# Expert blocks in first-need order, last combination and stores inside the second expert stage, block tables by matrix products

## Chip, cores and metric

The kernel runs on one core of one Trainium2 chip. The metric is device time in microseconds (us), median of three runs. A second number for the same kernel is the span of one profiled execution, from its first to its last instruction; the rows below come from that execution.

## What is computed

A layer of 8192 tokens (32 sequences of 256) with 128 features: a routed feed-forward, a linear attention, and the same feed-forward again.

```python
x = x + 0.5 * ffn(layernorm(x))      # 8 experts, top 2 of them per token, and a shared expert
x = x + attn(layernorm(x))           # linear attention over the 32 sequences, 16 heads of 8
x = x + 0.5 * ffn(layernorm(x))

def ffn(x):
    top_v, top_i = top_k(x @ gate_w, 2)
    top_p = softmax(top_v)
    d_e = (silu(x @ Wg[e]) * (x @ Wu[e])) @ Wd[e]            # 128 -> 352 -> 128
    return sum over the two chosen e of top_p * d_e  +  (silu(x @ Sg) * (x @ Su)) @ Sd
```

## The kernel before

Tokens go in 16 groups of 512 (GT), four tiles of 128 each; group g holds its x in X3(g), a slice of the resident tensor X. Every multiplication is made in a high and a low f16 part. The program has five stages, and all engines meet at the end of each (phase_end, L253).

1. Routing of the first feed-forward (first_ffn on each engine): logits, the two best experts, and a place for each of the 2 x 8192 token rows. DVE's place (L1215) adds running counts per expert (base) to positions that TensorE sums; the row of a token goes to its expert's region of the DRAM tensor routed_rows by an indirect DMA that POOL issues (scatter, L479, L485: eight per group). After the last group, ends and tables (L1244, L1249) make from the eight counts the tables of the expert stage: which row of routed_rows block b starts at (row_i) and which expert it belongs to (exp_i, eb).
2. Expert stage (experts on each engine): 72 places for blocks of 256 rows (NBLK), of which 71 are worked; the 16384 rows fill 64 blocks and each expert's last one is partly filled. Blocks are in the order of the experts: all of expert 0, then all of expert 1. For block n: SP loads it into one of four buffers (load_block, L372, L386), once block n-4 is transposed; TensorE transposes it (L983), makes gate and up products (18 matmuls of 256 columns, block_gate_up) and the down product of block n-2 (18 of 128, block_down); ACT takes silu (L683), makes the high part (L688) and copies the result of block n-2 out (L696, L697); DVE copies the transposed block (block_in, L1297), works out where its rows go (L1299), makes the low part of block n-1 (block_low, L1142) and the product of block n (block_mult, L1292); POOL writes a dummy (carrier, L494) and issues two indirect DMAs (L496) that scatter the 256 result rows of 512 bytes into the DRAM tensor expert_results, in the order of the tokens. ACT reuses a result buffer when the scatter of two blocks before has landed (s_results).
3. Streams: for each group, the two result rows per token are loaded and added, weighted with PR, then attention, then the routing of the second feed-forward. ends and tables again.
4. Expert stage, as 2, with n from 72 on.
5. Last combination: when every scatter has landed, SP loads group after group of result rows (load_last, 512 KB) into four buffers YL, ACT weighs the second choice (weigh_last, L665), DVE adds both (combine_last, L1345) and SP stores the group (store, L420, 256 KB). SP's order is: four loads, then store g, load g+4.

The order of the work on an engine is the order in which its program is written. DVE's step in the expert stage, which the change touches, is:

```python
def step(n, v, ahead=True):
    if ahead:
        block_in(n + 1, (v + 1) % XE, n + 1 - n0)
    block_low(n - 1, 1 - u)
    block_mult(n, u)
```

TensorE's step n is: transposes of block n+1 (which wait until DVE has copied block n out of the same PSUM bank, L979), gate and up of n, down of n-2.

## Time and profile before

| | |
|---|---|
| device time, median of three runs | 1241.1 us (1237.2, 1241.1, 1242.37) |
| the profiled execution, span | 1240.9 us |
| TensorE, busy | 989.7 us (80%), 8996 matmuls |
| VectorE (DVE), busy | 896.8 us (72%) |
| ScalarE (ACT), busy | 669.6 us (54%) |
| GpSimd (POOL), busy | 843.8 us (68%) |
| granted TensorE clock, mean | 0.930 |
| DMA | 86.62 MB, mean 70 GB/s |

How to read it: the profiled execution lies within 0.2 us of the median, so the sum can be made against its span. A busy share is an average over five stages with different limits; the table by stage is in the first group of rows below. Matmuls overlap in the record (their ends are modelled), so a step of TensorE is best read from the starts of its instructions. "issue" as a releaser means that the profile shows nothing that the engine waited for. A row of the engine "POOLq" or "DVEq" is the sequencer of that engine: register work, drains, waits.

### The profile page before, as it was taken

To read this page: it belongs to the slowest core of one execution; us is meant where nothing else is said; L and a number is where in the kernel's file an instruction comes from. 1 tells how busy PE (TensorE), PEld (TensorE's weight loads), DVE (VectorE), ACT (ScalarE), POOL (GpSimd) and SP (SyncE) were. 2 spreads that over 40 slices of the span, in tenths; PEclk is the share of its full clock that TensorE was granted. 3 is DMA by queue.
4 is the path that set the end of the run, shared out by engine and by line. 5 is a ranking of instruction groups with operands and counts; after the bars stand their busy time and mean duration, and the time that the engine had idled before them with its cause. 6 is when DMAs were issued, how large, how long until landed. Compare 5 with 4: busy or idle time off the path is not lost. (4 is left out here: it accounts for less than half of the span.)

```text
span 1240.9 us, 31979 instructions
## 1 busy us (share of the span) xinstructions
PE 989.7 (80%) x8996; PEld 742.7 (60%) x8997; DVE 896.8 (72%) x2369; ACT 669.6 (54%) x1466; POOL 843.8 (68%) x872
## 2 busy tenths in 40 slices
PE   2657665999999927788888888888864999999940
PEld 1434344899989924455555555555543888899930
DVE  6778784676676745788888888888854666666748
ACT  4556642555555523466665656666331555555545
POOL 4677773777777845467787787778642677777750
PEclk9898996999999968999999999999966999999985
DMA  9411122222222221001111111100003222222229
GB/s 279 108 51 47 52 76 66 78 79 76 78 77 78 68 59 33 17 33 37 34 34 51 34 38 41 41 17 18 23 27 87 74 74 77 78 75 78 73 95 332
DMA packets 68607, 86.62 MB, mean 70 GB/s; under 512 B 13004, under 2 KB 56209, under 8 KB 68558
## 3 DMA queue, kind: packets, MB, share of 16 engines
q1 hardware_dynamic: 51278, 52.15, 14.5%
q0 software_dynamic: 17280, 33.87, 8.3%
q8 instruction: 25, 0.41, 0.1%
q14 instruction: 24, 0.20, 0.1%
HBM read 44.74 MB, written 43.04 MB: 71 GB/s over the span
## 5 line engine op out<-in xcount | busy, mean ns | idle before, releaser
L496 POOL DMA_INDIRECT expert_results<-ey,eidx x284 | 293.3, 1033 | 70.9 <-issue 69.6
L485 POOL DMA_INDIRECT routed_rows<-row,idx x256 | 255.2, 997 | 73.6 <-issue 70.2
L1142 DVE SCALAR_TENSOR_TENSOR ehT<-eh,ehT 128x768 f16<-128x768 f32 x142 | 136.1, 958 | 150.1 <-ACT ehT L688 150.1
L683 ACT ACTIVATE esil<-PSUM 128x768 f32<-128x768 f32 x142 | 115.1, 810 | 230.2 <-PE PSUM L826 224.6
L824 PE MATMUL PSUM<-eT,WGU 128*128 128x256 f16 x852 | 234.3, 275 | 1.4
L825 PE MATMUL PSUM<-eT,WGU 128*128 128x256 f16 x852 | 233.9, 275 | 0.0
L826 PE MATMUL PSUM<-eT,WGU 128*128 128x256 f16 x852 | 233.8, 274 | 0.0
L510 POOL TENSOR_TENSOR space<-qk,val 128x1152 f32<-128x1152 f32 x64 | 138.2, 2171 | 69.5 <-DVE shift L1192 48.7
L824 PE MATMUL PSUM<-WD,ehT 128*128 x852 | 161.0, 220 | 8.3 <-DVE ehT L1142 5.0
L825 PE MATMUL PSUM<-WD,ehT 128*128 x852 | 159.3, 220 | 0.0
L826 PE MATMUL PSUM<-WD,ehT 128*128 x852 | 158.8, 219 | 0.0
L945 PE MATMUL PSUM<-space,upto 128*128 128x320 f32 (+1 forms) x384 | 148.4, 496 | 9.6 <-DVE prod L1366 6.8
L1292 DVE SCALAR_TENSOR_TENSOR eh<-PSUM,esil 128x768 f32<-128x768 f32 x142 | 134.9, 950 | 8.1 <-ACT esil L683 8.1
L494 POOL TENSOR_TENSOR carrier<-ones 128x1 f32<-128x1 f32 x142 | 73.0, 514 | 72.6 <-ACT ey L697 72.6
L688 ACT ACTIVATE ehT<-eh 128x768 f16<-128x768 f32 x142 | 118.6, 835 | 2.5 <-DVE eh L1292 2.5
L945 PEld LDWEIGHTS PSUM<-space,upto 128*128 128x128 f32 x384 | 71.8, 193 | 59.7 <-issue 42.0
L1366 DVE TENSOR_TENSOR prod<-PSUM,qk 128x1152 f32<-128x1152 f32 x64 | 86.3, 1348 | 13.9 <-PE PSUM L947 9.3
L824 PEld LDWEIGHTS PSUM<-eT,WGU 128*128 x852 | 83.7, 98 | 18.8 <-issue 6.8
L824 PEld LDWEIGHTS PSUM<-WD,ehT 128*128 128x128 f16 x852 | 82.9, 97 | 14.3 <-issue 9.7
L1369 DVE TENSOR_REDUCE space<-prod 128x144 f32<-128x1152 f32 x64 | 86.6, 1353 | 5.8
L826 PEld LDWEIGHTS PSUM<-eT,WGU 128*128 x852 | 84.0, 99 | 10.4
L825 PEld LDWEIGHTS PSUM<-eT,WGU 128*128 x852 | 84.1, 99 | 7.3
(197 smaller groups left out, 2300.0 us busy)
## 6 DMA issues: line engine op xcount, KB each, us to landing
xe<-routed_rows SPq DMA_DIRECT2D x142, 130.0 KB, 2.1
space<-expert_results SPq DMA_DIRECT2D x32, 512.0 KB, 3.9
expert_results<-ey,eidx POOLq DMA_INDIRECT x284
X<-in_L_attn_x_dram SPq DMA_DIRECT2D x16, 256.0 KB, 4.6
routed_rows<-row,idx POOLq DMA_INDIRECT x256, 2.3
out_dram<-X SPq DMA_DIRECT2D x16, 256.0 KB, 4.3
routed_rows<-pad_rows SPq DMA_DIRECT2D x24, 130.0 KB
space<-in_L_ffn_Wg_dram SPq DMA_DIRECT2D x1, 1408.0 KB, 9.1
```

What stands on the lines that cost most here:

```text
L485: pool.indirect_dma_start(routed, bass.IndirectOffsetOnAxis(ap=idx[u][:, k, j:j + 1], axis=0), row[u][:, j, :], None).then_inc(s_scattered ...
L496: pool.indirect_dma_start(result, bass.IndirectOffsetOnAxis(ap=eidx[u][:, h:h + 1], axis=0), ey[u][:, h, :], None, bounds_check=K * T - 1, ...
L510: pool.tensor_tensor(kv[:, q, a, :].rearrange("p (h j i) -> p h j i", h=HEADS, j=VD), k4, v4, ALU.mult).then_inc(s_outer, 1)
L683: act.activation(esil[u][:, :], PSUM[:, 1536 * u:1536 * u + 768], ACT.Silu, scale=2.0 ** -(SX + SWT)).then_inc(s_block_silu, 1)
L688: act.activation(ehT[u][:, 0, :, :], eh32[u][:, :].rearrange("p (c t) -> p c t", c=NC), ACT.Copy).then_inc(s_block_high, 1)
L824: pe.matmul(dst, a[0], b[0], start=start, stop=False)
L825: pe.matmul(dst, a[0], b[1], start=False, stop=False)
L826: return pe.matmul(dst, a[1], b[0], start=False, stop=stop)
L945: mm = pe.matmul(PKV[:, lo:hi], upto[:, :], kv[:, q, a, lo:hi], start=True, stop=(a == 0))
L1142: return dve.scalar_tensor_tensor(out=dst, in0=src, scalar=float(2 ** scale), in1=high, op0=ALU.mult, op1=ALU.subtract)
L1292: dve.scalar_tensor_tensor(out=eh32[u][:, :], in0=PSUM[:, at:at + NC * BLK], scalar=2.0 ** (SH - SX - SWT), in1=esil[u][:, :], op0=ALU.mul ...
L1369: dve.tensor_reduce(num[:, j, :, :], prod[:, a, :].rearrange("p (h j i) -> p h j i", h=HEADS, j=VD), AX.X, ALU.add)
```

## The change

**Tables.** The running counts are kept for every group (counts, 17 sets of 8, instead of base). For each pair of a group and an expert, the blocks that this group is the first to need are counted (fresh), pairs are ordered by group, then by expert, and two products on TensorE turn that into the starting row and the expert of each block. DVE's serial sum over eight experts and its four operations on 72 x 8 elements are gone; in their place stand three transposes and six products on TensorE, three round trips between the engines. TensorE does its part before down(14) in the first routing and before the last down in the second (tables(0), tables(1)).

**Last combination.** With blocks in this order, all result rows of group g are in DRAM when a first part of the blocks is through (COMPLETE + 1 + 4 g of them, in the code's terms). In the second expert stage SP loads and stores groups between block loads (merged), and DVE adds two pieces of a group per step: 128 x 128 of the first choice ahead of block_low, 128 x 128 of the second choice behind block_mult, after a drain. Four steps make a group; groups 0 to 12 are made in 52 steps, groups 13, 14 and 15 after the stage's end. ACT no longer weighs anything at the end.

```diff
+MERGED = 12
+COMPLETE = 10
...
+            def landed(g):
+
+                if not isinstance(g, int):
+                    sp.wait_ge(s_block_results, g * NJ + (NBLK + COMPLETE + 3))
+                    return
+                for u in range(2):
+                    sp.wait_ge(s_results[u], 16 * HALVES * (NBLK // 2 - u + COMPLETE // 2 + 1 - u + g * (NJ // 2)))
+
+            def merged(g, u, stored=True):
+                landed(g)
+                load_last(g, u)
+                if stored:
+                    store(g - 2)
...
-            for u in range(LAST):
-                load_last(u, u)
-            with sp.Fori(0, NG // LAST - 1) as i:
...
+            with sp.Fori(0, MERGED // LAST - 1) as i:
                 for u in range(LAST):
-                    store(i * LAST + u)
-                    load_last(i * LAST + (LAST + u), u)
-            for u in range(LAST):
-                store(NG - LAST + u)
+                    for v in range(XE):
+                        block_of(i * (LAST * XE) + (NBLK + 2 * LAST * XE + u * XE + v), v)
+                        if v == 2:
+                            merged(i * LAST + (LAST + u), u)
...
+            sp.drain().then_inc(s_phase, 1)
+            for g in range(MERGED + 2, NG):
+                merged(g, g % LAST)
+            for g in range(NG - 2, NG):
+                store(g)
             sp.wait_ge(s_stored, 16 * NG)
...
+            def tables(f):
+
+                pe.wait_ge(s_fresh, f + 1)
+                pe.transpose(PT[:, 0:P], fresh[:, :], ident[:, :])
+                pe.transpose(PT[:, P:2 * P], expert_step[:, :], ident[:, :]).then_inc(s_fresh_turned, 1)
+                pe.wait_ge(s_fresh_T, f + 1)
+                pe.matmul(SUM_BEFORE, turned[:, 0:P], before[:, :], start=True, stop=True)
...
+                pe.wait_ge(s_offsets_T, f + 1)
+                pe.matmul(SUM_OFFSET, offset_turned[:, :], past[:, :], start=True, stop=True).then_inc(s_block_sums, 1)
...
-                dve.tensor_tensor(base[:, :], base[:, :], pos[:, NJ, :], ALU.add)
+                dve.tensor_tensor(counts[:, cols(g, E, E)], old, pos[:, NJ, :], ALU.add)
...
-                def step(n, v, ahead=True):
+                def step(n, v, ahead=True, merge=None):
                     u = v % 2
                     if ahead:
                         block_in(n + 1, (v + 1) % XE, n + 1 - n0)
+                    if merge is not None:
+                        combine_last(*merge, 0)
                     block_low(n - 1, 1 - u)
                     block_mult(n, u)
+                    if merge is not None:
+                        dve.drain()
+                        combine_last(*merge, 1)
...
+                plain = LAST if f else (NBLK - 4) // XE
+                with dve.Fori(0, plain) as i:
                     for b in range(XE):
                         step(i * XE + (n0 + 2 + b), (2 + b) % XE)
+                if f:
+                    with dve.Fori(0, MERGED // LAST) as i:
+                        for g in range(LAST):
+                            for b in range(XE):
+                                step(i * (LAST * XE) + (n0 + LAST * XE + 2 + g * XE + b), (2 + b) % XE, merge=(i * LAST + g, g, b))
...
+            def combine_last(g, u, j, k):
+
+                if j == 0 and k == 0:
+                    dve.wait_ge(s_YL[u], (g - u) * (16 // LAST) + 16)
+                x1 = X3(g)[:, j, :]
+                last = dve.scalar_tensor_tensor(out=x1, in0=YL[u][:, j, k, :], scalar=PR[:, cols(g, NJ * K, j * K + k, 1)],
+                                                in1=x1, op0=ALU.mult, op1=ALU.add)
+                if j == NJ - 1 and k == K - 1:
+                    last.then_inc(s_combined, 1)
...
             phase_end(dve, 4)
-            with dve.Fori(0, NG // LAST) as i:
-                for u in range(LAST):
-                    combine_last(i * LAST + u, u)
+            for g in range(MERGED + 1, NG):
+                for k in range(K):
+                    for j in range(NJ):
+                        combine_last(g, g % LAST, j, k)
+                    dve.drain()
```

Two places show how the order moves. ISA and REGISTER_ALU rows are the sequencer's work on addresses and counters.

DVE, second expert stage, one step of the loop before (copy of the transposed block, its places, low part, product, and the copy of the next):

```order
L1297 COPY eT<-PSUM 128x512
L1299 ISA
L1299 SCALAR_TENSOR_TENSOR places<-xe,eb 128x2
L1142 SCALAR_TENSOR_TENSOR ehT<-eh,ehT 128x768
L1292 SCALAR_TENSOR_TENSOR eh<-PSUM,esil 128x768
L1296 REGISTER_ALU
L1297 COPY eT<-PSUM 128x512
```

DVE, the same step in the changed kernel's merging loop (X<-space,PR,X is a piece of the combination; space holds YL):

```order
L1350 COPY eT<-PSUM 128x512
L1352 ISA
L1352 SCALAR_TENSOR_TENSOR places<-xe,eb 128x2
L1416 ISA
L1416 SCALAR_TENSOR_TENSOR X<-space,PR,X 128x128
L1202 SCALAR_TENSOR_TENSOR ehT<-eh,ehT 128x768
L1345 SCALAR_TENSOR_TENSOR eh<-PSUM,esil 128x768
L1416 ISA
L1416 SCALAR_TENSOR_TENSOR X<-space,PR,X 128x128
L1349 REGISTER_ALU
L1350 COPY eT<-PSUM 128x512
```

One piece stands ahead of the low part, the other (with a drain that makes no row here) between the product and the copy of the next transposed block.

SP, second expert stage before: two block loads of the loop (xe), nothing between them:

```order
L251 REGISTER_ALU
L385 ISA
L385 TENSOR_LOAD row_i
L385 ISA x2
L386 ISA
L386 DMA xe<-routed_rows 128x260
```

SP in the changed kernel, between the third and the fourth block load of each four:

```order
L400 DMA xe<-routed_rows 128x260
L442 ISA
L413 ISA
L413 DMA space<-expert_results 128x1024
L435 REGISTER_ALU
L436 ISA
L436 DMA out_dram<-X 128x4x128
L265 REGISTER_ALU
L399 ISA
L399 TENSOR_LOAD row_i
L399 ISA x2
L400 ISA
```

A load of 512 KB and a store of 256 KB, each behind a wait, now stand in SP's queue ahead of every fourth block load.

## Rows read from the trace of the kernel before

**Rows 1.** Stages: from, to, length, busy us of each engine, PEclk, DMA share, GB/s.
```profile
197.90:450.90 253.00, 239.53 (x2840) 214.59 (x2840) 162.53 (x284) 137.28 (x284) 183.54 (x213) 0.97 0.25 71
...
947.40:1202.10 254.70, 240.33 (x2840) 213.97 (x2840) 162.93 (x285) 137.28 (x284) 182.66 (x213) 0.98 0.25 71
1202.10:1240.90 38.80, 0.00 (x0) 0.00 (x0) 28.76 (x80) 20.54 (x64) 0.00 (x0) 0.50 0.93 325
```

**Rows 2.** Timeline of DVE in the last stage (start, us, operation).
```profile
1209.74 1.13 DVE L1350 SCALAR_TENSOR_TENSOR X<-space,PR,X 128x128 f32 x4
1211.02 0.69 DVE L1354 TENSOR_TENSOR X<-X,space 128x512 f32 x1
...
1237.53 0.69 DVE L1354 TENSOR_TENSOR X<-X,space 128x512 f32 x1
```

**Rows 3.** Line 491, POOL's drain at a stage's last block: min/median/max ns, starts.
```profile
L491 POOLq DRAIN  x2: 4491/4779/5067, 448.5 to 1198.5; - x2
```

**Rows 4.** Timeline of DVE, start of stage 3: eight pieces of one group.
```profile
455.53 2.36 DVE L1339 SCALAR_TENSOR_TENSOR X<-space,PR,X 128x128 f32<-128x128 f32 x8 [1.93 <-DMA space<-expert_results]
```

**Rows 5.** Timeline of DVE, second expert stage, one step.
```profile
1062.82 0.41 DVE L1297 COPY eT<-PSUM 128x512 f16<-128x512 f16 x1
...
1064.31 0.96 DVE L1142 SCALAR_TENSOR_TENSOR ehT<-eh,ehT 128x768 f16<-128x768 f32 x1 [0.95 <-ACT ehT L688]
1065.19 0.95 DVE L1292 SCALAR_TENSOR_TENSOR eh<-PSUM,esil 128x768 f32<-128x768 f32 x1
1066.06 0.41 DVE L1297 COPY eT<-PSUM 128x512 f16<-128x512 f16 x1
```

**Rows 6.** Timeline of TensorE around the same step: its transposes.
```profile
1063.54 0.39 PE L983 MATMUL PSUM<-ident,xe 128*128 128x128 f16 x4
...
1066.97 0.39 PE L983 MATMUL PSUM<-ident,xe 128*128 128x128 f16 x4
```

**Rows 7.** Eight blocks of the second expert stage, columns as in rows 1.
```profile
1046.34:1073.07 26.73, 26.64 (x324) 23.84 (x321) 18.29 (x33) 15.34 (x33) 20.52 (x25) 1.00 0.27 77
```

**Rows 8.** POOL's timeline: a usual step, then steps behind a late one.
```profile
1064.73 0.59 POOL L494 TENSOR_TENSOR carrier<-ones 128x1 f32<-128x1 f32 x1 [0.21 <-ACT ey L697]
1065.47 1.00 POOL L496 DMA_INDIRECT expert_results<-ey,eidx  x1 [0.15 <-issue]
1066.78 0.98 POOL L496 DMA_INDIRECT expert_results<-ey,eidx  x1 [0.30 <-issue]
...
1155.60 0.98 POOL L496 DMA_INDIRECT expert_results<-ey,eidx  x1 [2.26 <-issue]
...
1161.37 1.50 POOL L496 DMA_INDIRECT expert_results<-ey,eidx  x1 [0.31 <-issue]
1162.86 0.24 POOL L494 TENSOR_TENSOR carrier<-ones 128x1 f32<-128x1 f32 x1
```

**Rows 9.** Waits of ACT, stages 2 to 4: us in total, times, longest.
```profile
ACT eidx L696 <- DMA expert_results<-ey,eidx: 4.7, 5, 2.0
```

**Rows 10.** Line 485, scatters of stages 1 and 3, issue to landing.
```profile
DMA to landing us min/median/max: 2.3/2.3/5.8
```

**Rows 11.** DMA issues of the last stage: count, KB each, median us to landing.
```profile
space<-expert_results SPq DMA_DIRECT2D x16, 512.0 KB, 5.0
```

**Rows 12.** Timeline of DVE, end of stage 3: first and last of the tables.
```profile
935.21 0.15 DVE L1251 TENSOR_TENSOR nb<-base,region 128x8 f32<-128x8 f32 x1
...
942.81 0.19 DVE L1285 CAST exp_i<-eb 128x72 int32<-128x72 f32 x1
```

**Rows 13.** The chain of waits from stage 3 into stage 4: start, us, what.
```profile
944.46 0.95 POOL routed_rows L485
...
946.95 3.34 POOLq L255
...
950.89 0.60 PE PSUM L983 x4
```

**Rows 14.** Line 1241: sequencer work on an address, min/median/max ns.
```profile
L1241 DVEq FUSED_REGOPS  x14: 57/57/76, 56.0 to 824.2; - x14
```

More of the change, by code:

```diff
@@ L125, in macaron @@
         block_no = sb("block_no", [P, NBLK])
-        base = sb("base", [P, E])
+        counts = sb("counts", [P, (NG + 1) * E])
         base_i = sb("base_i", [P, E], I32)
@@ L412, in _ @@
                     sp.wait_ge(s_scattered[v], scattered(f, v))
-                fours(sp, f * NBLK, (f + 1) * NBLK, load_block(f))
-                sp.drain().then_inc(s_phase, 1)
-                for u in range(2):
-                    sp.wait_ge(s_results[u], 16 * HALVES * (NBLK // 2 - u) * (f + 1))
                 if f == 0:
+                    fours(sp, 0, NBLK, load_block(0))
+                    sp.drain().then_inc(s_phase, 1)
+                    for u in range(2):
+                        sp.wait_ge(s_results[u], 16 * HALVES * (NBLK // 2 - u))
                     pairs(sp, 0, NG, load_results)
@@ L663, in weigh @@
                 last.then_inc(s_weighed, 1)
-            def weigh_last(g, u):
-                act.wait_ge(s_YL[u], (g - u) * (16 // LAST) + 16)
-                for j in range(NJ):
-                    last = act.activation(YL[u][:, j, 1, :], YL[u][:, j, 1, :], ACT.Copy,
-                                          scale=PR[:, cols(g, NJ * K, j * K + 1, 1)])
-                last.then_inc(s_weighed, 1)
             def residual(m):
@@ L1072, in first_ffn @@
                     pe.wait_ge(s_weights_low, 2)
+                if edge and n == NG - 1:
+                    tables(0)
                 if not edge or n > 0:
@@ L1105, in streams @@
                         qkv_products(m + 2, 1, a)
+                if isinstance(m, int) and m == NG:
+                    tables(1)
                 if settle:
@@ L1246, in ends, with tables @@
                 dve.drain()
-                dve.tensor_copy(base_i[:, :], base[:, :]).then_inc(s_row_ends, 1)
-            def tables():
-                dve.tensor_tensor(nb[:, :], base[:, :], region0[:, :], ALU.subtract)
-                dve.drain()
-                dve.tensor_scalar(nb[:, :], nb[:, :], float(BLK - 1), None, ALU.add)
+                dve.tensor_copy(base_i[:, :], counts[:, NG * E:(NG + 1) * E]).then_inc(s_row_ends, 1)
+            def tables(f):
+                dve.tensor_scalar(nb[:, :], counts[:, :], float(BLK - 1), None, ALU.add)
                 dve.drain()
@@ L1322, in experts @@
                 block_mult(n0 + 1, 1)
-                with dve.Fori(0, (NBLK - 4) // XE) as i:
+                plain = LAST if f else (NBLK - 4) // XE
+                with dve.Fori(0, plain) as i:
                     for b in range(XE):
                         step(i * XE + (n0 + 2 + b), (2 + b) % XE)
+                if f:
+                    with dve.Fori(0, MERGED // LAST) as i:
+                        for g in range(LAST):
+                            for b in range(XE):
+                                step(i * (LAST * XE) + (n0 + LAST * XE + 2 + g * XE + b), (2 + b) % XE, merge=(i * LAST + g, g, b))
+                    for b in range(XE):
+                        step(n0 + (LAST + MERGED) * XE + 2 + b, (2 + b) % XE, merge=(MERGED, 0, b))
                 step(n1 - 2, 2, ahead=False)
@@ L1425, in first_ffn @@
                     ends()
-                    tables()
+                    tables(0)
                 shared(n, 0)
@@ L1470, in _ @@
             dve.wait_ge(s_constants, 1)
-            dve.tensor_copy(base[:, :], region0[:, :])
+            dve.tensor_copy(counts[:, 0:E], region0[:, :])
             dve.wait_ge(s_second_tokens, 32)
@@ L1506, in streams @@
                         ends()
-                        tables()
+                        tables(1)
                     shared_low(n - 1)
```

100 lines of the change are left out of this document (61 added, 39 removed).

## The prediction

> **What bounds the kernel now.** I read the table by stage first. The last stage, in which TensorE and POOL do nothing, takes 38.8 us with the DMA engines 0.93 busy, and the two expert stages 253.0 and 254.7 us [rows 1] with DMA at 0.25: work of a loaded resource stands alone where the stages beside it leave it idle. Within an expert stage I then read eight blocks as one window: 26.73 us, so 3.34 per block, of which TensorE is busy 26.64, DVE 18.29, ACT 15.34 and POOL 20.52 [rows 7]. TensorE looks like the bound, but its matmul records overlap, so I checked by single steps how much later the others could be. DVE's timeline shows 0.95 us of idleness ahead of the low part, and none from the low part over the product to the copy of the next transposed block, which starts at 1066.06 and ends at 1066.47 [rows 5]. TensorE's next transposes wait for that copy and start at 1066.97; one step earlier the copy ended at 1063.23 and the transposes started at 1063.54 [rows 5, 6]. The slack is 0.3 to 0.5 us: a stage bound by TensorE, with DVE's chain right behind. The third view is POOL's timeline: it waited 0.21 us for ACT ahead of its dummy in a usual step, and after one issue that came 2.26 us late it no longer waits at all [rows 8]. So POOL is close behind too.
>
> **The last stage.** Removed are the 16 groups of loads, additions and stores, 38.8 us from the landing of the last scatter to the end [rows 1]. Put back are groups 13 to 15. DVE may not start them before all engines have met, and POOL comes last there: its drain begins at 1198.5 and takes 5.07 us [rows 3], to 1203.6; I take DVE's start as 1203.9. One group is eight pieces in 2.36 us [rows 4] and about 0.15 for the last drain (four pieces of 1.13 from 1209.74, the next operation at 1211.02: 0.15 behind them [rows 2]), 2.5 in all. Three make 7.5, to 1211.4. The load of group 15 starts when the last scatter has landed, at 1202.1, and with even 5.0 us [rows 11] is there by 1207.1, before DVE reaches it at 1208.9. From DVE's last operation to the end it was 2.7 us (1238.22 [rows 2] to 1240.9) and stays so. The end is then 1214.1: a gain of 26.8 us. The 13 other groups' loads and stores lie beside the expert stage.
>
> **What the merged steps cost.** In 52 of the 71 steps DVE makes two pieces more. The first stands in the 0.95 us of idleness [rows 5]; a piece takes 0.28 (1.13 / 4 [rows 2]), some 0.35 with its tail, and is covered, though with the copy coming later (below) only some 0.1 us of the cover is left. The second piece is on the chain: the product's start to the copy's start was 0.87 (1065.19 to 1066.06 [rows 5]); now it is 0.95 for the product to end, 0.15 of drain gap and 0.28, so 1.38, or 0.5 later. The slack was 0.3 to 0.5 less some 0.13 that a release takes (my estimate from the 0.1 to 0.15 between operations that follow each other), so 0.17 to 0.37. What is over, 0.13 to 0.33 us, delays the transposes of the block after next, so it is spread over two steps: 0.07 to 0.17 per block, 3.6 to 8.6 us over 52 steps. TensorE's clean step is shorter than the mean one of 3.34, and its own pauses take up some of it; I take 5.0, with 0 and 8.6 as the ends.
>
> **POOL and the scatters.** The dummy took 0.59 us with DVE's low part running beside it and 0.24 without, a scatter 1.50 against 0.98, and each time the longer one ends behind the end of the low part (1065.27; in the late steps likewise) [rows 5, 8]. So POOL is held up while DVE runs an operation on two SBUF inputs, and the new pieces are of that kind. This is the rule in the Trainium skill, SBUF — State Buffer, Who interferes with whom: a DVE instruction with two SBUF inputs and a GpSimd instruction that reads SBUF shut each other out for their whole length. The row agrees with the rule, and the rule speaks against the change. By itself it would have POOL lose both pieces in every step, which is the third case below; what the row adds is that a step loses only what meets a start. POOL's step is 0.24 + 0.15 + 1.00 + 0.30 + 0.98 without any of it, 2.7 us, and 3.0 with one hold-up, against 3.34; one more of 0.3 fits. I take 1 us for this, between 0 and 14.
>
> Beside that, the load of 512 KB and the store of 256 KB per group now share the DMA engines with the scatters. ACT waits for a scatter two blocks later; it did so 5 times for 4.7 us in all [rows 9]. Scatters landed in 2.3 us as a median and 5.8 at most [rows 10]; the second one of a block is issued at 1066.78 [rows 8], so it lands at 1069.1, and ACT, whose copy-out ended just ahead of the dummy at 1064.73, needs the buffer for the copy-out two steps or 6.7 us later, at about 1071: some 1.8 us are spare. I take 1 us, between 0 and 10. SP's queue: the fourth block load of each four stands behind a wait for a result, a load and a store. The wait is for the result of a block six places ahead of the last one loaded; that load itself was allowed when the block four places ahead was transposed, and its result comes two steps behind its transposes. So the fourth load comes about one step later than before; with four buffers it had three steps in hand, and the 0.77 MB in front of it take some 5 us of the rest. Nothing.
>
> **Tables and counts.** DVE's tables took 7.8 us (935.21 to 943.00 [rows 12]). The new ones have about 14 small operations at 0.25 us from start to start and three round trips over TensorE; I take 5.5 to 6 us. Neither is on the path: the stage ends with POOL's last scatter, at 945.41, its landing and POOL's drain of 3.34, while TensorE starts the next stage at 950.89 [rows 13]. The cover is POOL's eight scatters; without it the gain would be 2 us at either end of a routing. The pads and TensorE's down product, which stand behind the tables, come no later. So 0, for both. The running count now needs an address in each loop: 0.06 us [rows 14], once per group in 24 of 32 groups, 1.4 at most, 0.5 taken. POOL's two memsets and one iota more at the start are 0.7 us by the dummy's 0.24 [rows 8]; DVE and ACT normalize the first group meanwhile, so 0. The order of the blocks itself changes no duration: every block reads its expert by a register, before as after.
>
> **Sum.** 1240.9 - 26.8 + 5.0 + 1 + 1 + 0.5 = 1221.6 us. The executed profile stands 0.2 us under the median, which I leave out: 1221.5.
>
> **Rivals.** (a) The pieces are nearly free: TensorE's own pauses hide the 0.13 to 0.33 us, since DVE has 8 us of idleness in each eight blocks [rows 7]. Against it stands that this idleness lies in one place. Costs of 0 to 3: 1214 to 1217, say 1216. (b) POOL becomes the bound of the merged steps: with 3.3 us as in the late steps and one hold-up of 0.28 more, 3.6 per block, 0.26 x 52 = 14 us, with the address work 1229. For it: the late steps of 1155 and after, where POOL has no slack. (c) The pieces hold POOL up twice in every step, the low part does too, and the scatters land late behind the 768 KB: POOL needs 2.7 + 0.5 + 2 x 0.35 = 3.9 us per block, 0.56 x 52 = 29 us more than now. 1214.1 + 29 + 4 of landing = 1247, slower than before. It decides from 3.34 + 26.8 / 52 = 3.86 us per merged step. Against it: POOL's three reads and DVE's three long operations would all have to meet, in steps of one length. (d) The change does not do what it says: SP comes to its loads too late, DVE waits for YL in the middle of its loop, and the groups cost in the stage what they cost behind it. The load is issued some three steps ahead of its use and takes 5 us [rows 11] of 10, so it should not. It would bring half the gain back: 1235.
>
> **Chances and range.** My forecast (costs of 4 to 11 us, 1218 to 1225) 0.48; (a) 0.22; (b) 0.21; (c) 0.04; (d) 0.05. A measurement of this kernel tells 0.5% or 6.2 us from no change: faster is below 1234.9. That is the forecast, (a) and (b) whole, and a little of (d): 0.93; same 0.04, slower 0.03. The range takes in (a) and (b), down to all costs nought and up to POOL's case with 4 us of late scatters; since the three runs before lay up to 4 us under their median, it begins 2 us lower: 1212 to 1233.
>
> **What would show it.** In the changed profile: the last stage from the last scatter's landing to the end near 12 us, with three groups of eight pieces; DVE's piece behind the product 0.28 us and the copy starting 1.3 to 1.4 us behind the product's start; eight merged blocks as a window in 27.2 to 28.2 us; the 16 unmerged first ones as before; ACT's waits for scatters under 1 us per group. Wrong would be shown by waits of DVE for the loads of YL, by POOL without any wait for ACT in all merged steps at over 3.5 us, by TensorE waiting for the copy by over 0.3 us per step, and by the expert stage starting later behind the tables.

## The result, and the profile after

The changed kernel takes 1230.7 us as the median of four runs (1228.3 to 1232.5), the kernel before 1241.7 beside it: a ratio of 0.9926, 95% interval 0.9906 to 0.9945. The forecast of 1221.5 had the sign right and promised a gain of 19.6 us, where 11.0 came. The executed profile of the changed kernel is its quickest run, 1228.3 us with a span of 1226.5; as in every run here the time is some 1.8 us over the span. So the span before, 1240.9, stands for a time of 1242.7, 1 us over the median and not within 0.2 of it as was said there; the forecast gain isn't touched by this, but the two profiles lie 14.4 us apart where the medians lie 11.0. Where single runs took over 1.5% longer at a lower granted clock, as one of e4's six (1268.1 us), the ratios leave them out.

The windows by stage of the changed kernel, columns as in [rows 1]:

```profile
197.40:452.70 255.30, 240.49 (x2840) 214.99 (x2840) 162.55 (x284) 137.46 (x284) 183.23 (x213) 0.96 0.24 70
...
948.30:1214.95 266.65, 249.86 (x2840) 212.60 (x2840) 194.89 (x388) 136.92 (x284) 180.72 (x213) 0.97 0.36 110
1214.95:1226.50 11.55, 0.00 (x0) 0.00 (x0) 6.83 (x24) 0.00 (x0) 0.00 (x0) 0.50 0.36 114
```

Against [rows 1] the last stage fell from 38.8 to 11.55 us, and the second expert stage grew from 254.7 to 266.65, with DVE's busy time up by 32 us (104 pieces). All that lies outside these two stages is 0.9 us longer in this profile. The same 2840 matmuls of TensorE are busy 249.86 us in place of 240.33, so its idleness grew by only 2.4 us (16.8 against 14.4): where the ends of matmuls are modelled, a busy share doesn't show where 12 us are lost.

The timeline of DVE in two merged steps does (start, us, operation, in brackets the idle time before it and its releaser), beside [rows 5]:

```profile
1111.00 0.96 DVE L1202 SCALAR_TENSOR_TENSOR ehT<-eh,ehT 128x768 f16<-128x768 f32 x1 [0.36 <-ACT ehT L731]
1111.88 0.95 DVE L1345 SCALAR_TENSOR_TENSOR eh<-PSUM,esil 128x768 f32<-128x768 f32 x1
1113.03 0.35 DVE L1416 SCALAR_TENSOR_TENSOR X<-space,PR,X 128x128 f32 x1 [0.20 <-issue]
1113.29 0.42 DVE L1350 COPY eT<-PSUM 128x512 f16<-128x512 f16 x1
1113.63 0.21 DVE L1352 SCALAR_TENSOR_TENSOR places<-xe,eb 128x2 f32 x1
1113.76 0.34 DVE L1416 SCALAR_TENSOR_TENSOR X<-space,PR,X 128x128 f32 x1
1114.55 0.96 DVE L1202 SCALAR_TENSOR_TENSOR ehT<-eh,ehT 128x768 f16<-128x768 f32 x1 [0.45 <-ACT ehT L731]
```

The first piece (1113.76) is covered; DVE still waits 0.45 us for ACT behind it. The second (1113.03) is on the chain: the copy starts 1.41 us behind the product's start (1111.88), where it was 0.87. From ACT's silu of step 18 to that of step 66 of the second expert stage, counted from 0, the changed kernel takes 170.1 us, 3.545 a block, the kernel before 159.6, 3.325; these rows are the two ends of it:

```profile
1017.28 0.81 ACT L726 ACTIVATE esil<-PSUM 128x768 f32<-128x768 f32 x1 [1.78 <-PE PSUM L866]
...
1187.42 0.81 ACT L726 ACTIVATE esil<-PSUM 128x768 f32<-128x768 f32 x1 [1.41 <-PE PSUM L866]
```

0.22 us a block in 52 steps is 11.4 us. The waits of the changed kernel in that window (us in total, times, longest):

```profile
ACT esil L726 <- PE PSUM L866: 78.1, 48, 1.9
POOL carrier L545 <- ACT ey L740: 23.5, 44, 0.9
...
DVE ehT L1202 <- ACT ehT L731: 21.6, 48, 1.1
PEld PSUM L864 <- issue: 11.6, 37, 0.5
```

and of the kernel before in the same 48 steps:

```profile
POOL carrier L494 <- ACT ey L697: 13.0, 41, 0.7
...
PEld PSUM L824 <- issue: 1.8, 5, 0.4
```

POOL waits for ACT more than before, 23.5 against 13.0 us, so it sets no pace. No wait of DVE for YL appears, and none of ACT for a scatter. TensorE's pauses without a releaser were 5 and are 37, and all of them stand ahead of the tenth of the 18 weight loads of gate and up, where its queue loads the number of the next expert from memory (line 1047, between the gate and the up products):

```profile
1118.95 0.10 PEld L864 LDWEIGHTS PSUM<-eT,WGU 128*128 x1 [0.45 <-issue]
```

```profile
L1047 PEldq TENSOR_LOAD <-exp_i x142: 295/303/802, 200.0 to 1196.9; - x142
```

The load's 0.30 us was there before too. The reading is that the queue then had it behind it before the array needed the next product, and released later has not; e10 below tests it.

The end is what was forecast: the last load at 1214.95, POOL's drain, three groups of eight pieces, their stores.

```profile
1214.95 0.33 SPq L413 DMA_DIRECT2D space<-expert_results  x1
1216.54 7.25 DVE L1416 SCALAR_TENSOR_TENSOR X<-space,PR,X 128x128 f32<-128x128 f32 x24 [9.52 <-POOLq L269]
1218.93 5.27 SPq L436 DMA_DIRECT2D out_dram<-X  x3
```

### The profile page after: what moved, and what is told of

Its sections match the earlier page's. It is cut to its first block and busy times, and to the rows that moved or that the text cites. A ratio compares the mean times of both kernels' runs of the same rounds, so it can differ in the third digit from the quotient of the medians.

```text
span 1226.5 us, 31850 instructions
## 1 busy us (share of the span) xinstructions
PE 1002.4 (82%) x9014; PEld 744.1 (61%) x9015; DVE 901.5 (73%) x2403; ACT 649.2 (53%) x1402; POOL 839.6 (68%) x875
## 5 line engine op out<-in xcount | busy, mean ns | idle before, releaser
L547 POOL DMA_INDIRECT expert_results<-ey,eidx x284 | 288.6, 1016 | 71.2 <-issue 65.5
L536 POOL DMA_INDIRECT routed_rows<-row,idx x256 | 252.5, 986 | 73.5 <-issue 69.4
L864 PE MATMUL PSUM<-WD,ehT 128*128 x852 | 164.5, 220 | 9.5 <-ACT ey L740 5.5
L865 PE MATMUL PSUM<-WD,ehT 128*128 x852 | 161.8, 221 | 0.0
L866 PE MATMUL PSUM<-WD,ehT 128*128 x852 | 161.3, 220 | 0.0
```

The lines of the kernel that those rows point to most:

```text
L536: pool.indirect_dma_start(routed, bass.IndirectOffsetOnAxis(ap=idx[u][:, k, j:j + 1], axis=0), row[u][:, j, :], None).then_inc(s_scattered ...
L547: pool.indirect_dma_start(result, bass.IndirectOffsetOnAxis(ap=eidx[u][:, h:h + 1], axis=0), ey[u][:, h, :], None, bounds_check=K * T - 1, ...
L864: pe.matmul(dst, a[0], b[0], start=start, stop=False)
L865: pe.matmul(dst, a[0], b[1], start=False, stop=False)
L866: return pe.matmul(dst, a[1], b[0], start=False, stop=stop)
```

## The experiments

Ratios are to the kernel before on the same chip, with 95% intervals. "Step" is the time per block from the silu of step 18 to that of 66, as above. Three of the five sets (e5 to e8, e13 to e16, e17 and e18) ran on chips on which every kernel, the one before too, took some 11 to 12% longer; these have a part of their own.

**e1: both pieces ahead of the low part.**

```diff
 combine_last(*merge, 0)
+dve.drain()
+combine_last(*merge, 1)
 block_low(n - 1, 1 - u)
 block_mult(n, u)
-if merge is not None:
-    dve.drain()
-    combine_last(*merge, 1)
```

> The changed kernel with both pieces of the last combination ahead of VectorE's low part, in the time in which it waits for ScalarE anyway (0.45 us there in the changed kernel with one piece in it), so that nothing stands between the product and the next copy. Same number of pieces, same transfers, same tables. Theory 1 (the second piece makes the copy 0.54 us later, and TensorE's sequencer, not its array, runs out of lead): the copy starts 0.9 us behind the product's start again as before the change, the merged steps go back from 3.545 to 3.33 to 3.38 us a block, and the time falls from 1230.7 to 1220 to 1224 us. Rival (the pieces' transfers, the lock between VectorE and GpSimd, or VectorE's total of work slow the steps, wherever the pieces stand): the pace stays at 3.5, 1229 to 1232 us.

Measured: 1221.5 us, 0.9837 (0.9814 to 0.9861), step 3.368. Its DVE, one step:

```profile
1111.27 0.95 DVE L1345 SCALAR_TENSOR_TENSOR eh<-PSUM,esil 128x768 f32<-128x768 f32 x1
1112.13 0.41 DVE L1350 COPY eT<-PSUM 128x512 f16<-128x512 f16 x1
1112.46 0.21 DVE L1352 SCALAR_TENSOR_TENSOR places<-xe,eb 128x2 f32 x1
1112.60 0.34 DVE L1415 SCALAR_TENSOR_TENSOR X<-space,PR,X 128x128 f32 x1
1113.12 0.35 DVE L1415 SCALAR_TENSOR_TENSOR X<-space,PR,X 128x128 f32 x1 [0.17 <-issue]
1113.58 0.96 DVE L1202 SCALAR_TENSOR_TENSOR ehT<-eh,ehT 128x768 f16<-128x768 f32 x1
```

The copy is back at 0.86 behind the product. The same pieces and transfers at another place cost 0.04 us a block in place of 0.22, as theory 1 expected. DVE's wait for ACT is just used up by the two in this step. This kernel beats both kernels of the study, and has the lowest ratio of all that ran on chips like the first (e9's interval overlaps with its own).

**e2: the transfers without the pieces.** Seven of eight pieces of 13 groups are left out, so the combination is incomplete.

```diff
-    combine_last(*merge, 0)
...
-if merge is not None:
+if merge is not None and merge[2] == NJ - 1:
     dve.drain()
     combine_last(*merge, 1)
...
```

The piece that is left also makes DVE's wait for the load of the group.

> The changed kernel in which seven of eight pieces of each merged group are left out (the combination of 13 groups is incomplete); the last piece of each group stays as the signal for the store, so all loads and stores go on inside the expert stage as in the changed kernel. Theory 1: with a late copy in one step of four, 3.33 to 3.42 us a block, 1219 to 1223 us. Rival (the transfers of the merged groups slow the steps by contention): 3.5 us a block, 1229 to 1231 us.

Measured: 1227.7 us, 0.989 (0.9872 to 0.9908), step 3.480. Read by its time alone this would speak for the rival: it lies over theory 1's 1219 to 1223 us and just under the rival's 1229 to 1231, the step between both. The timeline says otherwise: the one piece left comes later than it did among eight, with 0.43 us of idleness for no releaser ahead of it (0.20 in the changed kernel), and the copy starts 1.64 us behind the product:

```profile
1092.39 0.95 DVE L1345 SCALAR_TENSOR_TENSOR eh<-PSUM,esil 128x768 f32<-128x768 f32 x1
1093.77 0.35 DVE L1414 SCALAR_TENSOR_TENSOR X<-space,PR,X 128x128 f32 x1 [0.43 <-issue]
1094.03 0.42 DVE L1350 COPY eT<-PSUM 128x512 f16<-128x512 f16 x1
```

From silu to silu, as means over the 48 steps by their place among four, beginning with the one in which the late copy lies:

```
us                   late copy     next    third   fourth    sum
before                   3.373    3.300    3.205    3.423  13.30
e2                       3.959    3.361    3.221    3.381  13.92
```

The loss of 0.62 us in four steps follows the one late copy (0.59, and 0.06 in the step behind it), and the other two run as before with all transfers going on. So the transfers are cleared, but by the timeline and e1, not by this time.

**e3: the kernel before with one piece on scratch memory**, in 52 steps of the second expert stage. No transfers, order and tables of before.

```diff
 block_mult(n, u)
+if piece:
+    dve.drain()
+    dve.scalar_tensor_tensor(out=prod[:, 0, 0:D], in0=prod[:, 0, 0:D],
+                             scalar=PR[:, 0:1], in1=prod[:, 0, D:2 * D],
+                             op0=ALU.mult, op1=ALU.add)
```

> The kernel before with one thing added: in 52 steps of the second expert stage VectorE makes a drain and one scalar_tensor_tensor of 128x128 on scratch memory behind the product, where the changed kernel has its second piece; no transfer, no new order, no new tables. Theory 1: the whole loss comes from this place alone, 0.18 to 0.24 us a step, 1241 + 9 to 12 = 1250 to 1253 us. Rival (transfers, order or tables): the added 0.45 us goes into the slack that the trace shows at TensorE, 1241 to 1243 us.

Measured: 1251.1 us, 1.0079 (1.006 to 1.0097), step 3.511, the copy 1.32 to 1.46 behind the product, and 34 pauses of TensorE ahead of the same tenth weight load. So a piece at this place, with no transfer and no new order or table, brings 0.19 of the 0.22 us; the rest is about what e1 still loses.

**e4: tables and order alone.** The changed kernel with the last stage of before (stores, combination and ACT's weighing behind the expert stage).

> The changed kernel's tables and order of the blocks, with the last combination and the stores behind the second expert stage as before. Theory 1: the order costs nothing in the steps, 3.32 to 3.34 us a block in both expert stages, and the tables nothing that is seen behind GpSimd's scatters: 1239 to 1242 us, as before the change. Rival (the new order, with its steps of expert number from block to block, makes the expert steps slower): 0.2 us more a block in the second stage, 1249 us or more.

Measured: 1245.9 us, 1.0041 (1.0025 to 1.0058), step 3.323. The order costs nothing in the steps, as expected; but the kernel is 3 to 7 us slower, which theory 1 had excluded, and not at the place that the rival named. From the last silu of the first expert stage to the first of the second it is 522.0 us against 518.7. In that middle stage the running count now stands at an address that depends on the group. The first three operations of place, in the kernel before:

```profile
757.50 0.19 DVE L1219 TENSOR_TENSOR posb<-PSUM,base 128x32 f32<-128x32 f32 x1 [1.26 <-PE PSUM L945]
757.76 0.16 DVE L1221 TENSOR_TENSOR base<-base,PSUM 128x8 f32<-128x8 f32 x1
757.84 1.12 DVE L1223 TENSOR_TENSOR pk<-pick,posb 128x64 f32<-128x64 f32 x1
```

and in e4:

```profile
758.14 0.19 DVE L1258 TENSOR_TENSOR posb<-PSUM,counts 128x32 f32<-128x32 f32 x1 [1.36 <-PE PSUM L979]
758.50 0.16 DVE L1260 TENSOR_TENSOR counts<-counts,PSUM 128x8 f32 x1 [0.17 <-issue]
758.58 1.08 DVE L1262 TENSOR_TENSOR pk<-pick,posb 128x64 f32<-128x64 f32 x1
```

```profile
775.00:776.00 1.00, 0.67 (x8) 0.49 (x9) 0.91 (x2) 0.85 (x5) 0.69 (x2) 1.00 0.01 4
776.00:777.00 1.00, 1.00 (x4) 0.51 (x3) 1.00 (x4) 1.00 (x6) 0.69 (x2) 0.57 0.19 62
777.00:778.00 1.00, 1.00 (x3) 0.67 (x2) 0.85 (x8) 1.00 (x5) 0.94 (x1) 0.50 0.20 67
778.00:779.00 1.00, 1.00 (x3) 0.67 (x2) 0.70 (x5) 0.98 (x3) 0.75 (x1) 0.50 0.19 67
779.00:780.00 1.00, 1.00 (x3) 0.53 (x2) 0.69 (x5) 0.99 (x2) 0.22 (x1) 0.72 0.19 67
```

Such a group, with a mean granted clock of 0.94, is in the profiles of the changed kernel, of e1, e9 and e10 (once each) and of e2 (twice), and not in those of the kernel before and e3, where it is 1.00. So it goes with the tables and counts; what makes the clock fall there is not shown.

A later group of the stage, in which the clock falls in the kernel before too, goes the other way. It has the same 88 matmuls in each kernel, before and changed (columns as in [rows 1]):

```profile
893.41:919.67 26.26, 17.47 (x88) 9.68 (x88) 16.63 (x51) 7.41 (x17) 9.05 (x10) 0.74 0.06 21
897.46:921.66 24.20, 14.69 (x88) 8.63 (x88) 16.62 (x51) 7.40 (x17) 9.08 (x10) 0.84 0.07 23
```

In e10 it has a clock of 0.91 and takes 22.9 us, in e4 0.74 and 26.3. So kernels with the same tables differ by up to 8 us between the two silus: e10 516.3, e9 518.4, the changed kernel 519.2, e4 522.0, e1 522.5, e2 524.4. One profile each doesn't tell how much of this is chance.

**e9: copies one block further ahead.** VectorE copies block m + 2 in step m, in its idle time ahead of the low part; the pieces stay.

```diff
-block_in(n + 1, (v + 1) % XE, n + 1 - n0)
+block_in(n + 2, (v + 2) % XE, n + 2 - n0)
```

(with the first and last steps of the loops shifted by one). 

> The changed kernel with VectorE's copies one block further ahead, once more, since the first time all kernels, the one before too, took 12% longer on that chip. In terms of the kernel before on the same chip: theory 1 (the chain of one step over the copy is cut) 0.982 to 0.985, the merged steps at 3.32 to 3.36 us where the kernel before has 3.33; the rival (the total of the pieces or the transfers) 0.990 to 0.994.

Measured: 1223.8 us, 0.9865 (0.9844 to 0.9886), between theory 1 and the rival. The steps without pieces became shorter than those of before (steps 18 to 66 of the first expert stage 3.290 against 3.313), the merged ones hardly, 3.537, where theory 1 expected 3.32 to 3.36. Its timeline shows a new chain:

```profile
1101.90 0.39 PE L1039 MATMUL PSUM<-ident,xe 128*128 128x128 f16 x4
1102.33 0.42 DVE L1350 COPY eT<-PSUM 128x512 f16<-128x512 f16 x1 [0.39 <-PE PSUM L1039]
...
1102.80 0.34 DVE L1415 SCALAR_TENSOR_TENSOR X<-space,PR,X 128x128 f32 x1
1103.06 0.95 DVE L1202 SCALAR_TENSOR_TENSOR ehT<-eh,ehT 128x768 f16<-128x768 f32 x1
...
1105.34 0.39 PE L1039 MATMUL PSUM<-ident,xe 128*128 128x128 f16 x4
```

Transposes, copy, places, first piece, low part, the down products that wait for it, next transposes: 3.44 us. By this reading the first piece is now on a chain. That is not shown: the kernels for it (e13, e17 below) ran on no chip like the first.

**e10: the expert's number loaded behind the up products.**

```diff
 for W, o in ((WG, 0), (WU, NC * BLK)):
-    if o and ahead is not None:
-        read_number(ahead, v)
...
 mm.then_inc(s_block_products, 1)
+if ahead is not None:
+    read_number(ahead, v)
```

> The changed kernel with the load of the next expert's number behind the up products, once more for the same reason. Theory 2 (the load sits in the chain of one step) 0.985 to 0.989 of the kernel before; if the late copy sets the pace wherever the load stands, 0.992 to 0.995. On the slower chip, whose queues show pauses everywhere, it had 0.967 where the changed kernel with another small edit had 0.987; that this is a gain of the slower chip alone would show here as 0.992.

Measured: 1226.8 us, 0.9883 (0.986 to 0.9905), step 3.500. A fifth of the loss of 0.22 comes back, 2.3 us in 52 steps of the 3.9 by which the medians differ. None of TensorE's pauses stands ahead of the tenth weight load of gate and up any more; 26 stand ahead of the down products. So the load is a part of the chain, the smaller one.

**e11 and e12: a fixed address for the counts, and all three edits.**

```diff
 def place(n, u, g):
+    dve.tensor_copy(counts[:, cols(g, E)], base[:, :])
     dve.wait_ge(s_positions, n + 1)
...
-    dve.tensor_tensor(counts[:, cols(g, E, E)], old, pos[:, NJ, :], ALU.add)
+    dve.tensor_tensor(base[:, :], base[:, :], pos[:, NJ, :], ALU.add)
```

> The changed kernel with both pieces ahead of the low part and, beside that, the running counts in a tile of fixed address, copied to the table in VectorE's idle time. The first alone had 0.984 of the kernel before. Theory 3 (the register work in the middle of place costs 2 to 4 us of the middle stage): 0.981 to 0.982 and no group of 29.2 us in the middle stage. Rival (it comes from elsewhere): 0.984.

> Both pieces ahead of the low part, counts in a tile of fixed address, and the load of the next expert's number behind the up products. If all three theories hold: 0.978 to 0.981 of the kernel before, below both kernels of this study; if the load only matters where the copy is late, it adds nothing to the other two, 0.981 to 0.983.

Measured: e11 1232.7 us, 0.9941 (0.9925 to 0.9957), step 3.367; e12 1228.1, 0.9907 (0.9888 to 0.9927), step 3.382. Both miss what was expected (0.981 to 0.984 and 0.978 to 0.983). Against e1 the fixed address made it worse. The middle groups take 27.8 us, with two and three of 29.1 to 29.5. The copy went to the wrong place: DVE's idle time is ahead of a wait for the running sums that stands before place, so the copy lies behind it.

```profile
627.28 0.55 DVE L1277 COPY counts<-base 128x8 f32 x1 [1.17 <-PE PSUM L1002]
627.75 0.18 DVE L1281 TENSOR_TENSOR posb<-PSUM,base 128x32 f32<-128x32 f32 x1
```

The copy and its address put 0.47 us between the release and the addition. It tells that DVE's chain bounds the middle stage and passes such a delay on, and nothing on theory 3. The load's place adds nothing once the copy is in time (3.382 against 3.367).

**On the slower chips.** There the kernel before took 1393 us (e5 to e8), 1374 (e13 to e16) and 1394 (e17, e18).

> The changed kernel with VectorE's copies one block further ahead in both expert stages: step m copies block m + 2 (not m + 1) before the low part of m - 1 and the product of m, so the copy that TensorE's next transposes wait for is done in VectorE's idle time and not behind the product and the second piece. Both pieces stay at their places. Theory 1 (a chain of one step: gate and up of m, silu, low part, product, second piece, copy of m + 1, transposes of m + 2, gate and up of m + 1; each step pays for the second piece anew): the chain is cut, 3.32 to 3.36 us a block in the merged steps, 1218 to 1223 us. Rival (not the copy but the total of the pieces or the transfers slow TensorE): 3.5 us a block, 1229 to 1232 us.

> The kernel before with the same change of VectorE's order in both expert stages and nothing else. TensorE was busy 159.1 of 159.6 us in 48 steps of the kernel before, so theory 1 expects nothing or the few tenths left there: 1238 to 1242 us. Rival (the copy already limits the steps of the kernel before, and the full array is only an effect of how ends are modelled): 0.1 us a block in 142 blocks, 1228 us or less.

> The changed kernel in which TensorE's queue loads the number of the next block's expert behind the up products and not between the gate and the up products; everything else as in the changed kernel. Theory 2 (the pauses of TensorE in the middle of gate and up, 0.24 us a step, are the register load that the queue no longer makes in time, and they are part of the chain of one step): without them 3.40 to 3.47 us a block, 1223 to 1227 us. Rival (the load only shows where the array runs dry, the late copy sets the pace wherever it stands): 3.5 us a block or more, 1229 to 1233 us.

> The changed kernel in which the running counts of place are kept in a tile of fixed address, as before the change, and are copied to the table of counts at an address by group in VectorE's idle time ahead of the wait for the positions. In the middle stage with the tables the groups took 27.5 us (27.4 before the change), and in each of four profiles one or two of them 29.2 with a drop of TensorE's clock in it; the kernel before and the one with a piece added to it show none. Theory 3 (the register work in the middle of place, 0.17 us of idleness there, is what puts 2 to 4 us on the middle stage): 1226.5 to 1229 us, no group of 29.2 us. Rival (the 4 us of the tables and the order come from elsewhere): 1230 to 1232 us.

Measured, as ratios: e5 (the edit of e9) 0.9893 (0.9848 to 0.9939), e6 (the same on the kernel before) 1.0025 (0.9992 to 1.0058), e7 (the edit of e10) 0.9674 (0.9622 to 0.9726), e8 (the fixed address alone) 0.9873 (0.9815 to 0.9932). The changed kernel did not run there, so e8 is the nearest to it.

> The changed kernel with VectorE's copies one block further ahead (as in the kernels copy_ahead) and both pieces behind the product, where VectorE now waits for the next transposes. With one piece ahead of the low part the merged steps had stayed at 3.54 us although the copy was off its old place, and the trace showed a new chain: transposes of m + 2, copy, places, first piece, low part, down products that wait for it, next transposes, 3.44 us. If that is the cause, taking the first piece out of it (0.26 us) lets TensorE's array set the pace: 3.29 to 3.33 us a block in merged and other steps, 0.977 to 0.981 of the kernel before, below both kernels. Rival (transfers or the total of VectorE's work keep the merged steps slow in this order): 3.45 to 3.54 us, 0.986.

> The changed kernel with both pieces ahead of the low part, and in place the update of the counts (with the register work for its address) behind the product of picks and positions and not ahead of it, so that GpSimd's index tile waits for the same number of operations but the address work lies beside one of them. Theory (the 0.09 us more from the positions' addition to that product is what makes the middle groups 27.5 and not 27.4 us): 27.4 us a group, 0.982 to 0.984 of the kernel before, against 0.984 for the one without this edit. Rival (the order does not matter, since the address work stands on VectorE's chain either way): no difference, 27.5 us a group.

> Both of the last two edits together: copies one block further ahead with both pieces behind the product, and the counts updated later in place. If both theories hold 0.975 to 0.980 of the kernel before; if only the first does, as that kernel alone.

> The kernel before with the piece on scratch memory behind the product doubled (drain and two scalar_tensor_tensor of 128x128 in 52 steps), so that the copy comes about 0.74 us later than before the change, after 0.46 with one piece (0.186 us a block lost) and 0.54 in the changed kernel (0.22 lost). A chain over two steps (copy of a block, its transposes' successor, gate and up, silu, low part, product, piece, copy of the block after next) with 0.1 us of slack loses half of what is over: (0.74 - 0.10) / 2 = 0.32 us a block, 1.013 to 1.014 of the kernel before. A chain over one step with 0.3 us of slack loses all of it: 0.44 us a block, 1.018 to 1.019.

> Copies one block further ahead and both pieces behind the product, once more, since the first time every kernel took some 11% longer on its chip and TensorE's queue paused in all of them. On a chip like the first: 3.29 to 3.33 us a block in merged and other steps, 0.977 to 0.981 of the kernel before. If the merged steps stay at 3.45 us or more, the chain over the first piece was not the cause, 0.986.

> The kernel before with two pieces on scratch memory behind the product in 52 steps, once more for the same reason. A chain over two steps with 0.1 us of slack: 0.32 us a block over the 3.33 of before in the merged steps, 1.013 to 1.014. A chain over one step with 0.3 us of slack: 0.44 us a block, 1.018 to 1.019.

Measured: e13 0.9857 (0.9815 to 0.99), e14 0.9719 (0.9669 to 0.9768), e15 0.9872 (0.9828 to 0.9915), e16 1.004 (1.0006 to 1.0073), e17 0.9837 (0.9804 to 0.9871), e18 1.0045 (1.001 to 1.008). The edits of the first two are

```diff
-combine_last(*merge, 0)
 block_low(n - 1, 1 - u)
 block_mult(n, u)
+combine_last(*merge, 0)
 dve.drain()
 combine_last(*merge, 1)
```

on top of e9, and on top of e1, in place,

```diff
-dve.tensor_tensor(counts[:, cols(g, E, E)], old, pos[:, NJ, :], ALU.add)
 dve.tensor_tensor(pk[:, :, :, :], pick[:, :, :, :], pb, ALU.mult)
 dve.drain()
...
+dve.tensor_tensor(counts[:, cols(g, E, E)], old, pos[:, NJ, :], ALU.add)
```

e15 has both, e17 is e13 again; e16 and e18 are e3 with a second piece behind the first. None of them decides what it was made for: steps take 2.5 to 7.0 us in one and the same loop (e18), and the means hide tenths. The two-piece kernel has 4.149 us a step in e18, and its 1.004 and 1.0045 miss both theories (1.013 to 1.014 and 1.018 to 1.019); why it loses less than e3 did on the first kind of chip is not shown. What these sets do show is in the last section.

## Why the prediction was wrong

**The last stage** was right: 11.55 us against "near 12", a gain of 27.2 against 26.8.

**The merged steps** are the step that failed: 5.0 us taken (0 to 8.6 as ends), 11.4 measured. Its parts can be read from the traces, as means over 44 to 46 of these steps, from the starts of the copy, the next transposes (T), the silu behind them, the product behind that, and the copy behind that:

```
us                  copy to T  T to silu  silu to product  product to copy    sum
before                  0.911      2.420            2.449            0.868  6.648
e1 (pieces ahead)       0.953      2.446            2.450            0.868  6.717
e3 (before + piece)     0.698      2.529            2.450            1.358  7.036
changed                 0.659      2.563            2.451            1.430  7.103
e10 (load later)        0.725      2.391            2.451            1.430  6.997
```

The sum is two steps in each kernel (before 2 x 3.325, changed 2 x 3.55): the chain returns to the copy after two steps. So "spread over two steps" was right, and the expectations of e5 and e9, which speak of a chain of one step, have this wrong; e16 and e18, made to settle it, weren't needed for it. "0.5 later" was right (0.56). The slack was 0.25 us in the gap between copy and transposes (0.911 to 0.659), inside the 0.17 to 0.37 that [rows 5, 6] had given. By these alone the loss is (0.56 - 0.25) / 2 x 52 = 8.1 us, near the upper end; the 5.0 came of letting "its own pauses take up some of it", for which no row stood, and that was the first fault. The second is a term that was put at nothing: the stretch from T to silu was taken as fixed and grew by 0.143 us, 3.7 us in 52 steps. That is the register load that the queue makes while the array waits: with the load moved, e10 has 2.391. Slack was read where the array starts; the queue in front of it had less. 8.1 + 3.7 is 11.8, beside 11.4 measured. The signs named for a wrong forecast did not tell it: DVE never waited for YL in these steps, POOL waited for ACT in 44 of 48, TensorE for a copy once, 0.2 us. Only the eight merged blocks, 28.4 us (8 x 3.545), lay just outside the 27.2 to 28.2.

e2 fits the same chain. Even and odd blocks are two chains side by side, so a piece in each step costs once per two steps (0.455), four steps 0.91. A single copy 0.77 us late in four steps costs 0.62, all but 0.15; that it does so on its own chain alone is argued, not shown.

**POOL and the scatters**, 1 + 1 us: nothing of it is seen. POOL's wait for ACT grew by 10.5 us, and in the whole second expert stage ACT waited once, 1.4 us, for a scatter. The mutual exclusion that the Trainium skill states (SBUF — State Buffer, Who interferes with whom) may still lengthen single operations. The dummy takes 0.56 us as a mean in that stage, in place of 0.53, a scatter 1.00 in place of 1.03, and nothing shows in their sum: POOL is busy 180.72 us in the second expert stage in place of 182.66 [rows 1], with 104 more operations of DVE beside it, and e1 has the same pieces at 0.04 us a step. POOL does not set the pace here, so this has no price.

**Tables and counts**, 0 + 0.5 us: 3 to 7 measured in e4, 0.5 in the changed kernel's own profile. The tables are in fact hidden. From the first to the last of them DVE takes 5.5 us, with POOL's scatters going on for over 4 us more and its drain behind (timeline of DVE, then the chain of waits):

```profile
936.68 0.22 DVE L1312 TENSOR_SCALAR nb<-counts 128x136 f32<-128x136 f32 x1
...
941.95 0.26 DVE L1338 CAST exp_i<-eb 128x72 int32<-128x72 f32 x1
```

```profile
945.77 0.96 POOL routed_rows L536
...
948.22 3.34 POOLq L269
```

What failed in e4 is the address of the counts: its 0.06 us [rows 14] was priced right, twice in place and at 0.10 together, at most 1.5 us in the stage, but not the clock drop of 1.8 us that goes with it, nor some 0.7 us more in one of the last groups (27.4 in place of 26.8). That is up to 4.0, where e4's profile is 3.3 longer there. The changed kernel has all of this too, but its late group got 2.1 us back at a clock of 0.84 in place of 0.74. So the middle stage of its profile is only 0.5 us longer (519.2 against 518.7), and whether its other runs paid as e4's did is not shown.

Together: in the two profiles -27.25 for the last stage, +11.95 for the second expert stage and +0.9 for the rest are the 14.4 us between the spans. By the medians, 1241.8 - 27.2 + 11.4 + 3.8 (e4's five runs other than that of 1268.1 us, against before) = 1229.8, beside 1230.7; that it comes so near is in part luck, since the 3.8 is e4's. Of the rivals, (a) is what e1 does, not this kernel; (b) and (c) fall with POOL's waits, (d) with the missing waits for YL. That (b) named nearly the right time, 1229, was an accident of its price.

Open stay: what makes the clock fall in the middle stage, and so what tables and counts cost from run to run; whether the first piece holds e9's merged steps; whether a later update of the counts helps.

## What to carry to other kernels

Slack read at an engine's array is not the slack of its queue: where the queue works out addresses or loads registers within the stretch, a later release lengthens the stretch itself, so add that work to the delay or test it with an operation on scratch memory (e3). Before a small piece is put into a loop, follow each chain of waits until it returns to itself and put the piece where its engine waits for something that is not on that chain: here 0.04 in place of 0.22 us a step, for two moved lines. When a kernel without the suspected work is still slow, look at where the remaining work went before believing it (e2).

## What the runs showed of the hardware

- The kernel before took 1241 to 1242 us on two chips and 1374 to 1394 on three others, with the same durations of single operations: a low part 0.95 to 0.96 us on either kind. The same edit ran on both kinds in e9 (1221.3 us in its profile) and e5 (1375.6). Of the 154 us between them 47 lie ahead of the first silu, 50 and 53 in the expert stages and 4 in the middle. What grew most are pauses ahead of TensorE's weight loads for which no releaser shows, those of line 864 in e9 and in e5:

```profile
PEld PSUM L864 <- issue: 28.4, 52, 3.6
```

```profile
PEld PSUM L864 <- issue: 148.5, 159, 6.0
```

  In e17 they come back at the same places of TensorE's loop of eight steps; these two are 33.9 us or eight steps apart:

```profile
1180.34 0.10 PEld L864 LDWEIGHTS PSUM<-WD,ehT 128*128 128x128 f16 x1 [1.29 <-issue]
...
1214.22 0.10 PEld L864 LDWEIGHTS PSUM<-WD,ehT 128*128 128x128 f16 x1 [1.29 <-issue]
```

  The DMA queues of kind "instruction" moved as many packets in e5 as in e9 (25 and 27), so it is not that more of these were needed. Why these chips have the pauses, and whether it is the chip or a state that it was in, is not shown.
- What an edit is worth depends on the chip. On a slower one, e14 (pieces ahead of the low part) had 0.972 and e15 (copies further ahead, pieces behind the product, the same late counts) 0.987 in one set, with intervals apart; on the chips like the first, e1 had 0.984 and e9 0.987, with overlapping ones. e7, with only the load moved, had 0.967 on a slower chip, the same edit (e10) 0.988 on one like the first.
